# Turning the softmax's weights in a fused attention and expert kernel: by way of DRAM and VectorE instead of TensorE

## The reference

```python
def attention(h, ctx, Wq, Wk, Wv, Wo, bo):        # 16 heads of 64
    q, k, v = h @ Wq, ctx @ Wk, ctx @ Wv
    scores = einsum('bhsd,bhkd->bhsk', q, k) / 8
    probs = softmax(scores, axis=-1)
    return einsum('bhsk,bhkd->bhsd', probs, v) @ Wo + bo

def experts(x, gate_w, fc1, b1, fc2, b2):         # 8 experts, top 2, capacity 1024 each
    scores = softmax(x @ gate_w.T); topv, topi = top_k(scores, 2)
    # each token goes to a slot of its experts, in order, as far as capacity goes
    h = relu(rows @ fc1.T + b1); eo = h @ fc2 + b2
    return weighted sum of a token's two results

x = x + tanh(g_xattn) * attention(layernorm(x), ctx_768, ...)   # x: 32 x 128 x 256, ctx: 32 x 128 x 192
x = x + tanh(g_ffn) * experts(layernorm(x), ...)
```

## Time and profile before

| what | value |
|---|---|
| median of 3 runs | 937.44 us (937.43 to 938.58) |
| profiled execution, own time | 935.3 us |
| its span, first to last instruction | 933.6 us |
| granted TensorE clock, mean | 0.996 of full speed |
| TensorE busy | 916.7 us, 98% of the span |
| VectorE, ScalarE, GpSimd busy | 72%, 56%, 30% |
| DMA | 73.36 MB, mean 79 GB/s |

### The profile page before, as it was taken

The page is one execution under the profiler, slowest core; times in us unless marked ns, Lnnn a source line. Parts: engine busy times, 40 slices in busy tenths (PEclk is TensorE's granted clock), DMA queues, the critical chain, the costliest instruction groups (busy, mean ns, idle before and its releaser), DMA issues.

```text
span 933.6 us, 18948 instructions
## 1 busy us (share of the span) xinstructions
PE 916.7 (98%) x7104; PEld 800.9 (86%) x7104; DVE 670.4 (72%) x1566; ACT 519.6 (56%) x1608; POOL 276.8 (30%) x300
## 2 busy tenths in 40 slices
PE   8999999999999999999999999999999999999996
PEld 6788889889889889889888887999999999999995
DVE  4885795895895885885965864777777767777762
ACT  5774683783774783784764742535454453535331
POOL 5911124133133133233132152222222223242322
PEclk9999999999999999999999999999999999999998
DMA  7195320121121021012011015654444445363322
GB/s 248 39 311 134 114 70 29 42 69 35 36 70 40 30 75 57 8 63 75 1 36 57 7 68 157 121 110 91 97 90 98 94 93 132 56 147 45 50 23 23
DMA packets 124379, 73.36 MB, mean 79 GB/s; under 512 B 76910, under 2 KB 117141, under 8 KB 124288
## 3 DMA queue, kind: packets, MB, share of 16 engines
q1 hardware_dynamic: 112000, 55.89, 22.6%
q0 software_dynamic: 12288, 16.25, 9.0%
HBM read 43.23 MB, written 29.49 MB: 78 GB/s over the span
## 4 chain that ended last, share of the span: by engine, by line
PE 92%; DVE 3%; issue 1%; ACT 1%; POOL 1%; DMA 1%; POOLq 0%; DVEq 0%; SPq 0%
PE out_bank L612 7%; PE probT L599 7%; PE down L1433 6%; PE down L1434 6%; PE down L1435 6%; PE score L624 6%; PE up L1419 6%; PE up L1420 6%; PE up L1421 6%; PE query_bank L540 3%; PE query_bank L542 3%; PE query_bank L541 3%; PE key_bank L566 3%; PE key_bank L558 1%; PE value_bank L576 1%; PE key_bank L560 1%
## 5 line engine op out<-in xcount | busy, mean ns | idle before, releaser
L1355 POOL DMA_INDIRECT out_dram<-eo,index x64 | 100.1, 1564 | 261.1 <-DVE eo L1558 233.0
L1475 ACT ACTIVATE hid<-up,b 128x512 f32<-128x512 f32 x124 | 85.5, 690 | 154.2 <-PE up L1421 102.2
L1076 DVE TENSOR_REDUCE negmax<-score 128x4 f32<-128x512 f32 x128 | 82.3, 684 | 41.8 <-PE score L624 41.7
L814 ACT ACTIVATE k_sb<-key_bank 128x512 f32<-128x512 f32 x64 | 38.7, 604 | 118.1 <-PE key_bank L566 116.9
L862 ACT ACTIVATE probs_odd<-score,negmax 128x128 f32<-128x128 f32 x256 | 91.3, 383 | 20.7 <-DVE negmax L1076 20.7
L439 POOL DMA_INDIRECT disp<-packed,slots x56 | 56.8, 1014 | 153.8 <-DMA disp<-packed,slots 100.2
L862 ACT ACTIVATE work<-score,negmax 128x128 f32<-128x128 f32 x256 | 91.4, 384 | 16.8 <-DVE negmax L1076 16.1
L1084 DVE COPY pT<-probT 128x512 f32<-128x512 f32 x128 | 82.2, 683 | 14.7 <-PE probT L599 14.6
L1548 DVE TENSOR_TENSOR hid_l<-hid,hid_h 128x512 fp32r<-128x512 f32 x128 | 88.6, 692 | 4.4
L1546 DVE CAST hid_h<-hid 128x512 fp32r<-128x512 f32 x128 | 55.0, 430 | 37.7 <-ACT hid L1475 37.3
L624 PEld LDWEIGHTS score<-k_sb,q_sb 64*128 64x128 f32 x1024 | 66.7, 187 | 5.6 <-ACT q_sb L814 3.1
(11 more groups left out here) (320 smaller groups left out, 2744.2 us busy)
## 6 DMA issues: line engine op xcount, KB each, us to landing
disp<-fixed SPq DMA_DIRECT2D x1, 8256.0 KB, 33.2
rows<-x_dram SPq DMA_DIRECT2D x16, 512.0 KB, 5.2
w_raw<-fc1T_dram SPq DMA_DIRECT2D x8, 1024.0 KB, 5.9
w_raw<-fc_dram SPq DMA_DIRECT2D x8, 1024.0 KB, 9.6
blocks<-disp SPq DMA_DIRECT2D x120, 64.0 KB, 3.3
out_dram<-rows SPq DMA_DIRECT2D x8, 512.0 KB, 3.2
c_raw<-ctxT_dram SPq DMA_DIRECT2D x8, 256.0 KB, 4.4
c_raw<-ctxT_dram SPq DMA_DIRECT2D x16, 128.0 KB, 4.7
```

The lines of the kernel that those rows point to most:

```text
L1076: V.tensor_reduce(negmax[:, w % 2, hh * GB:(hh + 1) * GB], score[hh][:, :].rearrange("p (i k) -> p i k", i=GB), axis=AX, op=ALU.max, negat ...
L1355: pool.indirect_dma_start(out=out_rows[:, :], out_offset=bass.IndirectOffsetOnAxis(ap=index[half][:, i:i + 1], axis=0), in_=eo[half][:, i, ...
L1475: nc.scalar.activation(hid[m % 2][:, :], up_bank(n, m)[:, :], ACT.Relu, bias=b1[par][:, m:m + 1]).then_inc(s_hid, 1)
```

## The change

The weights of steps 0 to 60 (`BOUNCED = STEPS - 3`) are no longer turned by TensorE. SP stores the scaled `probs` of a step to a DRAM tensor `weights` (two DMAs of 256 KB, one for each `hh`), waits until each store has landed, and loads them back in blocks of 32x32 (eight DMAs of 64 KB, the shape of L1324) into `blocks`, which lies in `w1_raw`. VectorE turns the blocks into `pT` (`turn_probs`) in place of the copy out of PSUM. TensorE turns only the last three steps' weights. The weighted sums move from two steps behind to three, and the projection, the transposes and the routing of a group (`MISC`) one step later. The values run one step ahead and no longer two, and the front transposes use the banks `probT` that are now free. The clearing of `disp` becomes eight DMAs (steps 1 to 8), and expert 0's first layer is loaded after the last block load, since `w1_raw` is in use until then.

The constants and SP's queue:

```diff
-V_AHEAD = 2
+V_AHEAD = 1
-MISC = {2: ["O0", "O1"], 3: ["XA", "XB"], 4: ["LT"], 5: ["LX"], 6: ["PR"]}
+MISC = {3: ["O0", "O1"], 4: ["XA", "XB"], 5: ["LT"], 6: ["LX"], 7: ["PR"]}
+BOUNCED = STEPS - 3
+BLANKS = 8
...
+    blocks = [w1_raw[:, par, :].rearrange("p (h t) -> p h t", h=2) for par in range(2)]
...
+        def bounce(w):
+
+            for hh in range(2):
+                sp.wait_ge(s_p_ready, 2 * w + hh + 1)
+                if w > 1:
+                    sp.wait_ge((s_pt_done0, s_pt_done1)[hh], w - 1)
+                sp.dma_start(weights[w % 2, hh].rearrange("(b p) k -> p b k", p=P),
+                             probs[w % 2][:, hh * GB:(hh + 1) * GB, :]).then_inc(s_store[hh], 16)
+            for hh in range(2):
+                sp.wait_ge(s_store[hh], 16 * (w + 1))
+                sp.sem_inc(s_probs_out, 1)
+                for q in range(P // SQ):
+                    sp.dma_start(blocks[w % 2][q * SQ:(q + 1) * SQ, hh, :].rearrange("s (t d) -> s t d", d=SQ),
+                                 weights[w % 2, hh][:, q * SQ:(q + 1) * SQ].rearrange("(t s) d -> s t d", s=SQ)).then_inc(
+                                     s_blocks[hh][w % 2], 16)
+
+        def step(u):
+
+            g, j = divmod(u, NP)
+            if u == 1:
+                sp.wait_ge(s_w_lo, 3)
+                sp.wait_ge(s_w_rest, 2)
+            if 0 < u <= BOUNCED:
+                bounce(u - 1)
+            if g < NG - 1 and j == 0:
+                sp.wait_ge(s_f_ready, 2 * g + 2)
+                load_x(g + 1, 0, s_x_in)
+            if g > 0 and j == 0:
+                if g > 1:
+                    sp.wait_ge(s_o_done, 2 * g - 2)
+                load_x(g - 1, 1, s_xr_in)
+            if g < NG - 2 and j == (4, 1)[min(g, 1)]:
+                sp.wait_ge(s_c_ready, g + 2)
+                load_ctx(g + 2)
+            if 1 <= u <= BLANKS:
+                sp.wait_ge(s_blank, 1)
+                rows_of = slice((u - 1) * E * CAP // BLANKS, u * E * CAP // BLANKS)
+                sp.dma_start(disp[rows_of, :].rearrange("(t p) w -> p t w", p=P),
+                             blank[:, :].unsqueeze(1).to_broadcast([P, E * CAP // BLANKS // P, W])).then_inc(s_blank_out, 16)
+            if u == BLANKS + 2:
+                sp.wait_ge(s_w_rest, 4)
+                load_second_layer(sp, fc2, 0, w2_raw, s_e0_in)
+            if g > 0 and j == 5:
+                store(g - 1, g)
...
+        for u in range(STEPS):
+            step(u)
+        for done in (s_pt_done0, s_pt_done1):
+            sp.wait_ge(done, BOUNCED)
+        load_first_layer(sp, fc1T, 0, w1_raw, s_e0_in)
```

TensorE, in `step(u)` and in `finish()`:

```diff
-            kinds, w, i = misc_of(u), u - 2, u + V_AHEAD
-            if w >= 0:
-                transpose_probs(w)
+            kinds, w, i = misc_of(u), u - 3, u + V_AHEAD
             query(u)
...
+            if u % NP == NP - 1 and u + 1 < STEPS:
+                pe.wait_ge(s_xn_ready, u // NP + 2)
+                for k in range(DK):
+                    front(probT[k], k)
...
+            transpose_probs(STEPS - 3)
+            project_pairs((3,), (1,))
+            pe.wait_ge(s_pr_done, NG - 1)
+            project_pairs((0, 1), (0,))
+            pe.wait_ge(s_at_split, STEPS - 3)
+            weigh_values(STEPS - 3)
+            project_pairs((2, 3), (0,))
             transpose_probs(STEPS - 2)
```

ScalarE, in `exponentials(w, hh)`:

```diff
+            if 1 < w < BOUNCED + 2:
+                act.wait_ge(s_probs_out, 2 * (w - 2) + hh + 1)
```

VectorE, the new helper and its place in `step(u)`:

```diff
+        def turn_probs(w):
+
+            if w > 0:
+                dve.wait_ge(s_av_ready, w)
+            for hh, pt_done in enumerate((s_pt_done0, s_pt_done1)):
+                dve.wait_ge(s_blocks[hh][w % 2], 16 * (P // SQ) * (w // 2 + 1))
+                V.transpose(pT[:, hh, :], blocks[w % 2][:, hh, :]).then_inc(pt_done, 1)
...
-            if u > 1:
-                probs_out(u - 2)
...
             if u > 0:
                 scale_probs(u - 1, 0)
+            if u > 3:
+                attention_low(u - 4)
             if u > 2:
-                attention_low(u - 3)
+                turn_probs(u - 3)
```

More of the change, by code:

```diff
@@ L91, in gated_block @@
     disp = nc.dram_tensor("disp", [E * CAP, W], f32, kind="Internal").ap()
+    weights = nc.dram_tensor("weights", [2, 2, TOK, P], f32, kind="Internal").ap()
     x_v = x.rearrange("b p d -> p b d")
@@ L117, in gated_block @@
         with ExitStack() as ctx:
-            attention(nc, ctx, block, sem, x_v, out_v, disp, ctxT, g_x, g_f, wq, wk, wv, wo, bo, gateT, fc1T, fc2, shared)
+            attention(nc, ctx, block, sem, x_v, out_v, disp, weights, ctxT, g_x, g_f, wq, wk, wv, wo, bo, gateT, fc1T, fc2, shared)
         with ExitStack() as ctx:
@@ L139, in load_expert, with attention @@
     load_second_layer(sp, fc2, e, w2_raw, done2)
-def attention(nc, ctx, block, sem, x_v, out_v, disp, ctxT, g_x, g_f, wq, wk, wv, wo, bo, gateT, fc1T, fc2, shared):
+def attention(nc, ctx, block, sem, x_v, out_v, disp, weights, ctxT, g_x, g_f, wq, wk, wv, wo, bo, gateT, fc1T, fc2, shared):
     f32, f32r, i32, u32 = mybir.dt.float32, mybir.dt.float32r, mybir.dt.int32, mybir.dt.uint32
@@ L223, in attention @@
         "dve_self", "pool_self", "dve_gate", "pool_gate", "e0_in", "c0_hi", "e0_hi", "gc_ready", "gc_done",
-        "shift", "shift2", "before", "lt_ready", "lt_done", "second", "minus_mean", "pair_in", "beat",
+        "shift", "shift2", "before", "lt_ready", "lt_done", "second", "minus_mean", "pair_in", "beat", "probs_out",
     ))
+    s_store = [sem(f"a_store{hh}") for hh in range(2)]
+    s_blocks = [[sem(f"a_blocks{hh}{par}") for par in range(2)] for hh in range(2)]
     s_wv_in, s_wq_in, s_wk_in = ([sem(f"a_{n}_in{half}") for half in range(2)] for n in ("wv", "wq", "wk"))
@@ L311, in _ @@
         load_ctx(1)
[L312 to L318, removed]
-        load_expert(sp, fc1T, fc2, 0, w1_raw, w2_raw, s_e0_in, s_e0_in)
-        for g in range(2, NG - 1):
-            iteration(g, g + 1, True)
-        iteration(NG - 1, None, True)
-        sp.wait_ge(s_o_done, 2 * NG - 2)
-        load_x(NG - 1, 1, s_xr_in)
+        for u in range(STEPS):
[3 more added lines that the diff above has]
+        load_first_layer(sp, fc1T, 0, w1_raw, s_e0_in)
         store(NG - 1, NG + 1)
```

101 lines of the change are left out of this document (44 added, 57 removed).

## The result

The changed kernel takes 1025.09 us (median of 4 runs, 1023.25 to 1028.88), the kernel before 937.43 us (937.30 to 938.58): a ratio of 1.094, 95% interval 1.090 to 1.097. The forecast was 985 us, with a range of 940 to 1,050. Direction and range held; the forecast was 40 us short, and the experiments show that its main step was wrong, so that part of this is luck. The profiled execution took 1023.25 us, its span is 1021.4 us, 87.8 us more than before.

The account below looks back on a forecast made before the run. TensorE, busy 98%, bounds the kernel; afterwards SP's queue would. Start 25, 60 turns 462, clearing 33, expert 0's second layer 4, x 24, contexts 11, x1 11 give 570 us; the attention's end adds 48 to 937.4: 985 us, range 940 to 1,050.

Parts of the forecast that it names:

- SP's turn: SP's queue, per step: two stores, 3.0 us until landing, eight loads 4.6 us, 0.1 us for waits; 7.7 us together.
- What is removed: TensorE's transposes in the attention: 0.87 us a step, 53 us for 61 steps; a plain step falls to 5.70 us.
- What is moved at no cost: VectorE's turning replaces its PSUM copy, under 1 us difference; sums, projection and routing one step later are the same instructions.
- The end of the attention: After the last steps: one more set of weighted sums, +1.0 us; expert 0's first layer's low part moved for nothing.
- rival 2: SP's turn shorter by the DMA fixed-cost rule: store lands in 2.6 us, turn 7.3 us, time 961 us; chance 0.17.
- SP's work is continuous: SP's queue in the long step: that step does not help, a stock of two steps only lets SP continue through it.
- SP, not TensorE, sets the pace: Attention groups: SP needs 69.0 us for a group for which TensorE needs 60.0 us.
- The clearing: Group 0, clearing of disp in SP's queue: eight parts of 4.1 us, each followed by an awaited store, 33 us.
- Rival 1: TensorE stays the attention's bound, faster: about 913 us, or 885 us without the clearing's loss; chance 0.14.
- rival 4: Whole kernel comes out even, TensorE's gain meeting the clearing's loss; chance 0.02.
- Rival 3: DMA engines become the bound: a turn of 8.2 us and more, time above 1,015 us; chance 0.22.

Follow-up runs that it names:

- e1: Changed kernel without the stores and loads of the weights, so the attention's output is not computed: 953.95 us, beside 937.37 before.
- e6: e1 with the statistics of the next group's x one step later and their normalising in j = 5: 939.24 us.
- e9: e6 with ScalarE copying the scaled query ahead of the odd head's exponentials: 927.92 us, beside 935.59 before.
- e12: e10 with VectorE's gate logits moved from before the even head's scaling to behind the odd head's: 943.23 us, ratio 1.0082.
- e10: Changed kernel, full computation, with e3's order, e2's load, TensorE turning steps 0 to 7, e6's later statistics and e9's query move: 939.37 us, ratio 1.0034.
- e2: Changed kernel with the load of the next group's x issued ahead of the turn in SP's queue: 999.23 us.
- e4: Changed kernel with the eight DMAs that clear disp issued by ScalarE instead of SP: 1013.0 us.
- e7: Changed kernel with the weights of steps 0 to 7 turned by TensorE and DMAs only from step 8 on: 985.01 us.
- e3: Changed kernel with SP's order interleaved: store even, load the previous step's odd head, store odd, load even: 994.63 us.
- e5: e1 with the scaled query ahead of the odd exponentials and the high and low parts of the sums behind them: 964.8 us.

## Why the prediction was right and wrong

The forecast said: TensorE's step falls to 5.70 us, SP's turn of 7.7 us becomes the bound, and the difference is 48 us. The direction is right, but not by that way: in groups 2 to 6 every step but j = 2 and 3 is about as long as in e1, where SP moves no weights, so SP's turns did not set their pace; and TensorE's step did not fall to 5.70 us. Measured are +56.5 us for the arrangement, where the forecast had +1, -40 for the transposes, where it had -53, and +71 for the DMAs, where its 48 leaves +100. The first term is 55 us too low, the second promised 13 too much, and the last is 29 too high: that they came within 40 us of the time is in part luck.

**What is removed: wrong.** "A plain step would be 5.70 us, and a group 67.0 - 8 x 0.87 = 60.0 us." No run shows that. With all DMAs of the weights gone (e1) a plain step takes 6.33 us and a group 69.3 us, 2.3 us more than before instead of 7 less. I took TensorE's 98% and the busy times of the others, VectorE 5.41 and ScalarE 4.97 us of 6.57 in the earlier trace rows, as their bounds. But busy time is not a loop's length: through three engines with their waits it was 6.34 us. The edits show what was there to win: 14.7 us by the later statistics (e6), 9.7 by the loop (e9). Even so the gain without any DMA of the weights is 7.7 us, not 53.

**What is moved at no cost: wrong, and the costliest error of reasoning.** That the instructions are the same is true; but one step later they meet others. In j = 4 VectorE has 7.8 us to do (6.0 before), in j = 7 8.7 us (7.5 before). e6 shows that for j = 4 by experiment; for j = 7 e12 failed, so that its cause stays open. VectorE's busy time there is not only more instructions: one of them, the routing mask, now falls beside GpSimd's work and takes 1.31 us where it took 0.22 (see the last section).

**The end of the attention: too low.** The one more set of weighted sums was counted as +1.0 us, and the low part of expert 0's first layer was counted as nothing; the part behind the scores of step 63 grew by 6.6 us. All of it lies before the first product of the experts, which comes 47.9 us after these scores in place of 41.3; the experts take 359.6 us in both. The last weighted sums come 3.4 us later, the last scatter 5.5. In e1 the first product of the experts comes after 48.0 us, so it is not the weights' DMAs. Which of the moved pieces it is was not tried.

**SP's turn: right in its parts, slightly long.** From a store's issue to the first load it took 2.5 to 3.9 us in most turns (forecast 3.0), the eight loads 4.04 to 4.07 us in half of the bursts (forecast 4.6), and the turns with none of these held up took 6.7 to 7.4 us (forecast 7.7). The row for 512 KB and the Trainium skill's rule (page "DMA: Bandwidth & Descriptors", section "Anatomy of one DMA — SWDGE (gpsimd) path"), which gave 2.6 us for 256 KB, both bear on this; the medians of 2.7 and 2.8 us in e10 are near the rule's 2.6, although the section states it for DMAs that GpSimd issues, and these are SP's. So rival 2 had the turn right. But its 961 us did not follow, since the turn's length did not set the time of the later groups.

**"SP's work is continuous", "SP, not TensorE, sets the pace": wrong.** By the undisturbed turn of 7.0 us, with the forecast's 7.4 us for the rest, SP would need 8 x 7.0 + 7.4 = 63.4 us in a group (an estimate), and a group took 75 us. SP waits for VectorE in the long step (the turns of steps 18, 26 and 34 took 14.0, 13.3 and 13.4 us) and behind `x` (those of 24, 32 and 40: 11.9, 12.9 and 10.9 us). That the forecast's 69.0 us a group lies beside e1's 69.3, where SP has no weights to move, is chance. What it lacked was who waits for `x`: I had priced its two loads as 3.7 us of SP's queue, and not asked for whom they come late. That is VectorE, with 35.8 us of waiting, and through it all engines; e2 gives 26 us back.

**The clearing: right in size.** 8 x 4.1 = 33 us in the queue were foretold, and turns of about 11.8 us; turns 1 to 7 are 10.6 to 12.3 us. That it costs by its place in SP's queue is shown for a part only (9 us of the two groups in e4). By the same sum the weighted sums in step 16 would end at 25 + 13 x 7.7 + 33 + 3.7 + 9.2 + 12.1 = 183 us; step 17 started at 178.6. So up to there the forecast was 4 us too long, and from there on (399 us foretold, 437.5 measured) 38 us too short. That is the miss, and it lies in groups 2 to 6: 75.5 us each where 69.0 stood, by j = 2. Group 7, for which VectorE waits for no next `x`, is as long as before.

**The rivals.** Rival 1 (TensorE stays the bound, 885 to 913 us) is out: even with no DMA of the weights e1 took 954 us and e9 928. So is rival 4. Rival 3 (1,015 us and more) has the right time for another reason: the DMA engines' share in group 4 is 0.27 to 0.76, and from 24 to 69 us, beside the clearing, 0.78; they were not full, and e2 takes 26 us off without moving a byte less.

**What stays open.** The 71 us that come with the DMAs are, by the steps of the profiles, 39 us in groups 0 and 1, of which e7 takes 35, and 29.5 us in groups 2 to 6, of which e2 takes 21. e3 takes 14 us off each of the two parts, so it overlaps with both, and no run gives SP's waiting inside the turn alone. Open are also j = 7, and the 6.6 us at the end of the attention.

## What to carry to other kernels

Before counting what a removed instruction gives back, walk once round the loop that joins one step to the next, through every engine and its order, and take its length: that is the step's next bound, and busy shares do not show it. When work moves by a step, list for each in-order engine what it then stands beside, and for each DMA who waits for it behind a newly inserted wait. A wait that was moved out of one engine's way (e5, e12) was paid by the next engine in the loop; only e9's edit took it out of the loop.

## What the runs showed of the hardware

- TensorE stood without work from 342.6 to 348.1 us, and its granted clock fell: the stretch 338.71 to 352.05 has a mean clock of 0.75, the second half of it (345.4 to 352.1) at the lower of its two levels (1.2 and 2.4 GHz). The scores' 16 products took 2.08 us there, against 1.05 us at 388.56; TensorE's busy time in the group is 63.5 us against 61.8 in e1. So this stall cost TensorE another 1.7 us behind itself.
- A burst of eight loads of 64 KB took 4.04 to 4.07 us in 32 of 61 turns, 505 ns for each load, and never less. That SP's issuing sets this is argued from the equal lengths; no run has loads of another size or number. With the clearing issued by ScalarE it was up to 7.68 us (e4).
- Moving 8 MB of clearing to another engine's queue gave 12 us (e4); keeping the turns away from it gave 40 (e7).
- Beside a GpSimd elementwise instruction some two-input operations of VectorE stretched. The routing mask of 128x64 took 0.22 to 0.23 us in all seven groups of the kernel before, with no GpSimd instruction beside it. In the changed kernel it took 1.31 to 1.32 us in five groups, each time beside a `TENSOR_TENSOR` of GpSimd that had begun some 0.05 us earlier, and 0.22 to 0.23 in the two with none. It ends with its neighbour. The rows are e12's:

```profile
331.99 1.29 POOL L427 TENSOR_TENSOR c_d<-c_raw,c_t 128x512 fp32r<-128x512 f32 x1
...
332.04 1.32 DVE L1065 TENSOR_TENSOR mask<-iota,choice 128x64 f32<-128x64 f32 x1
```
